# Query sets written and read in pairs, idle products, and the first feed-forward products inside the attention's end

## The reference

```python
x = x + layernorm(attention(layernorm(x), Wqkv, Wo))          # 32 heads of 16, one shared key and value head, ALiBi, causal
x = x + layernorm(ffn(layernorm(x), gate, up, down))          # weights of 4 bits, 512 -> 1376 -> 512
x = x + layernorm(layernorm(x) @ (weight * blockmask).T + bias)
x = x + layernorm(base + 0.5 * fourier(encode(layernorm(x))))  # folded into one 512 x 512 matrix

def ffn(x):      # Wg, Wu, Wd = (code - (zero + 1)) * scale, a zero and a scale for each group of 128 rows
    return (silu(x @ Wg) * (x @ Wu)) @ Wd
```

## Time and profile before

| | |
|---|---|
| median of 3 runs | 1154.56 us (1153.49 to 1155.82) |
| the profiled execution | 1155.38 us |
| its span, first to last instruction | 1153.6 us |
| PE busy | 1095.1 us, 95% of the span |
| DVE, ACT, POOL busy | 62%, 54%, 37% |
| mean granted clock of PE | 0.986 |

### The profile page before, as it was taken

One profiled execution on the slowest core, in us unless ns is written; L12 is line 12 of the kernel. 1 busy time (PEld: TensorE's weight loads), 2 busy tenths in 40 slices (PEclk: granted clock), 3 DMA queues, 4 the chain that ended last, 5 costly groups with the idle time before them and its releaser, 6 DMA issues.

```text
span 1153.6 us, 16292 instructions
## 1 busy us (share of the span) xinstructions
PE 1095.1 (95%) x5822; PEld 678.7 (59%) x5888; DVE 717.3 (62%) x1675; ACT 624.1 (54%) x1067; POOL 423.1 (37%) x494
## 2 busy tenths in 40 slices
PE   7699999999999999899998899999999999999997
PEld 7445346345334334334535667788878878777885
DVE  6597997996999999799622644251141151247674
ACT  5265875766778689987794434211111111136775
POOL 4364252354210634322265655221121121124765
PEclk8799999999999999999999999999999999999999
DMA  6416104003213012101310221330030032211101
GB/s 184 131 43 166 29 20 119 21 20 77 62 38 101 22 35 64 58 29 47 95 37 28 75 64 39 110 110 1 1 110 1 1 79 101 74 37 74 37 37 74
DMA packets 66349, 70.62 MB, mean 61 GB/s; under 512 B 39854, under 2 KB 45510, under 8 KB 64708
## 3 DMA queue, kind: packets, MB, share of 16 engines
q1 hardware_dynamic: 62540, 59.82, 17.4%
q0 software_dynamic: 3152, 8.63, 2.3%
q10 hardware_dynamic: 576, 1.11, 0.3%
HBM read 50.27 MB, written 18.87 MB: 60 GB/s over the span
## 4 chain that ended last, share of the span: by engine, by line
PE 78%; DVE 11%; ACT 5%; issue 2%; POOL 2%; DMA 1%; SPq 1%; POOLq 0%; DVEq 0%; ACTq 0%
PE PO L1511 10%; PE ST L1497 8%; PE bank L1413 8%; PE f_pair L61 7%; PE f_pair L63 7%; PE f_pair L62 7%; DVE bank L1207 3%; PE f_Y L1906 3%; PE f_Y L1908 3%; PE f_Y L1907 3%; ACT PT L1119 3%; PE l_psum L2331 2%; PE l_psum L2333 2%; PE l_psum L2332 2%; DVE mx L1209 2%
## 5 line engine op out<-in xcount | busy, mean ns | idle before, releaser
L1119 ACT ACTIVATE PT<-ST,lowered 128x512 f32<-128x512 f32 x576 | 355.1, 693 | 72.6 <-PE PO L1511 31.7
L1207 DVE CUSTOM_DVE_ANT_0 bank<-bank,tail_mask 128x512 f32<-128x512 f32 x320 | 211.1, 719 | 21.2 <-PE bank L1413 20.9
L1413 PE MATMUL bank<-KS,QS 125*128 125x512 bf16 (+2 forms) x896 | 179.4, 307 | 10.2 <-DMA QS<-q_scratch 4.7
L1497 PE MATMUL ST<-QS,KS 128*128 128x512 bf16 x523 | 170.2, 384 | 11.0 <-ACT PT L1119 4.3
L1209 DVE TENSOR_REDUCE mx<-bank 128x2 f32<-128x512 f32 (+2 forms) x256 | 161.1, 681 | 25.9 <-PE bank L1413 11.4
L1037 POOL TENSOR_SCALAR_AFFINE_SELECT PT<-PT 128x512 f32<-128x512 f32 x128 | 79.2, 646 | 220.3 <-ACT PT L1119 219.7
L1511 PE MATMUL PO<-PT,V 128*32 128x512 f32 x1152 | 152.6, 604 | 2.9 <-ACT OT L1132 1.7
L1832 DVE TENSOR_TENSOR f_h<-f_h,f_pair 128x512 f32<-128x512 f32 (+1 forms) x44 | 30.2, 687 | 194.8 <-ACT f_h L1776 194.8
L1776 ACT ACTIVATE f_h<-f_pair 128x512 f32<-128x512 f32 (+1 forms) x44 | 26.3, 598 | 217.1 <-PE f_pair L63 217.1
L1736 POOL TENSOR_TENSOR f_h_part<-f_h,f_h_part 128x512 fp32r<-128x512 f32 (+1 forms) x44 | 56.7, 1289 | 232.0 <-ACT f_h_part L1780 232.0
L61 PE MATMUL f_pair<-f_xT,gw 128*128 128x512 f32 (+1 forms) x352 | 139.9, 398 | 0.0
(11 more groups left out here) (210 smaller groups left out, 1799.0 us busy)
## 6 DMA issues: line engine op xcount, KB each, us to landing
QS<-q_scratch SPq DMA_DIRECT2D x96, 128.0 KB
q_scratch<-QP SPq DMA_DIRECT2D x36, 128.0 KB, 1.9
xres<-_attn_hidden_states_dram POOLq DMA_DIRECT2D x16, 256.0 KB, 3.3
x_dram<-xout POOLq DMA_DIRECT2D x16, 256.0 KB, 2.4
xin<-x_dram SPq DMA_DIRECT2D x4, 1024.0 KB, 7.7
f_xsum<-x_dram SPq DMA_DIRECT2D x4, 1024.0 KB, 7.0
x_dram<-f_xsum SPq DMA_DIRECT2D x4, 1024.0 KB, 4.7
out_dram<-l_xout SPq DMA_DIRECT2D x7, 512.0 KB, 2.8
```

What stands on the lines that cost most here:

```text
L1119: act.activation(PT[:, quad % PT_RING, n % 4, :], ST[:, n % ST_RING, :], ACT.Exp, bias=lowered[:, 0:1]).then_inc(p_done, 1)
L1207: v.tensor_tensor_reduce(at(u), at(u), tail_mask[:, :], 1.0, -3e38, ALU.add, ALU.max, mx[:, i % 2, z, h:h + 1]).then_inc(bank_free_dve, 1)
L1413: last = pe.matmul(at(u)[:, j * w:(j + 1) * w], QS[0:ROWS1, slot, h + j, :], KS[b][0:ROWS1, k0:k0 + w], start=(j == 0 or not diag), stop=( ...
L1497: pe.matmul(ST[:, n % ST_RING, :], KS[b][0:ROWS2, kb * P:(kb + 1) * P], QS[0:ROWS2, slot, h:h + 4, :], start=True, stop=True).then_inc(st_ ...
```

## The change

- **Sets.** The six sets stand in `QS` grouped by the query part (48 rows of part 0, then 32, then 16) and no longer interleaved, and a block's stack is three DMAs, each with a source that is read three, two or one times. `QP` is laid out by token tile, so that two groups m lie side by side, and a part is sent to `q_scratch` in pairs of m: six DMAs a piece in place of twelve, each of twice the bytes in runs of 512 B in place of 256 B. The key weights are copied in five groups rather than three. ACT, DVE and POOL write and read `QP` with a stride between token tiles.
- **Opening.** 13 products of zeros at the start in place of 12, and five more after the first two transposes. POOL waits with its second part of the weights (chunk 3) until DVE has done its first (`wx_lo` at 1).
- **The planner** knows of eight steps "ff" of three matmuls each, the gate and up products of tile 0 of block 0, which may run once all score tiles are issued and read, into banks 0 and 1 of `ST`, at the lowest rank. Its figures for SP's issues and the stacks are changed.
- **Feed-forward, block 0.** Tile 0's gate and up products are gone from it. Then follows one piece, and from tile 1 on gate, piece, up, piece, down of the tile before, piece. ACT takes silu between the copy and the high part of the second piece. DVE takes the row moments one tile of tokens at a time beside n = 1 to 4, and the normalising beside n = 5 to 8; it did all four beside n = 1 and n = 2. A gate or up product waits for the low parts of its weights chunk by chunk. Some counts of waits on SP are one lower.

```diff
-WARM_UP = 12
+WARM_UP, WARM_TURN = 13, 5
...
-def pieces_during(n):
-    p = n // 2 + 1
-    mine = [j for j, (u, _) in enumerate(DQ) if UNITS[u][0] == p]
-    return mine[0:3] if n % 2 == 0 else mine[3:6]
+def between(n):
+    extras = [("dq", j) for j, (u, _) in enumerate(DQ) if UNITS[u][0] > 0] + [("xt", t) for t in range(4)]
+    return extras[max(0, 3 * n - 2):3 * n + 1]
...
+        if at["ff"] < FF_STEPS and at["tile"] == 4 * QUADS:
+            m = at["ff"] // DC
+            made = [("dl", j) for j in EARLY_PIECES if UNITS[DQ[j][0]][1] <= m]
+            out.append((known(("read", 4 * QUADS - 1), ("xt", AFTER, 3), *made), free["pe"] + 9000, ("ff", at["ff"])))
...
-        KV_GROUPS = ((0, SETS, D), (SETS, 1, D + HD), (SETS + 1, P // HD - SETS - 1, D))
-        Q_OUT = 4 * 16
+        KV_GROUPS = tuple((PART_ROW[x] // HD, PART_SETS[x], D) for x in range(PARTS)) + ((SETS, 1, D + HD), (SETS + 1, P // HD - SETS - 1, D))
+        Q_OUT = 2 * 16
...
-                sp.dma_start(q_scratch[b, t:t + n, part, :, :, m].rearrange("t d h q -> (d h) t q"),
-                             QP[:, part, m, cols_of(k)].rearrange("p (t q) -> p t q", q=P)).then_inc(q_out[part], 16)
+                sp.dma_start(q_scratch[b, t:t + n, part, :, :, m - 1:m + 1, :].rearrange("t d h m q -> (d h) t (m q)"),
+                             QPv[:, part, tiles_at(k), m - 1:m + 1, :].rearrange("p t m q -> p t (m q)")).then_inc(q_out[part], 16)
...
-                for g in range(SETS):
-                    if Q_PART[g] == part:
-                        sp.dma_start(QS[g:SETS * HD:SETS, slot, :, :].rearrange("d h q -> d (h q)"),
-                                     q_scratch[b, qb, part].rearrange("d h m q -> d (h m q)")).then_inc(qs_in[slot], 16)
+                n, r = PART_SETS[part], PART_ROW[part]
+                sp.dma_start(QS[r:r + n * HD, slot, :, :].rearrange("d h q -> d (h q)"),
+                             q_scratch[b, qb, part].rearrange("d h m q -> d (h m q)").unsqueeze(1).to_broadcast([HD, n, NH * P])).then_inc(qs_in[slot], 16)
...
-            for m, part in ((0, 0), (1, 0), (0, 1), (0, 2), (2, 0), (1, 1), (1, 2), (3, 0), (2, 1), (2, 2), (3, 1)):
+            for m, part in ((1, 0), (1, 1), (1, 2), (3, 0), (3, 1)):
                 q_part_out(0, m, part)
             stack_part(0, 0)
             q_part_out(0, 3, 2)
...
             weights_low(0)
             piece_rstd(0)
+            pool.wait_ge(wx_lo, 1)
             weights_low(DC - 1)
...
+            def first_tile(x):
+                m, c = divmod(x, DC)
+                if x == 0:
+                    freed(pe, ("xt", AFTER, 3))
+                    pe.wait_ge(p_done, 4 * QUADS)
+                if c == 0:
+                    pe.wait_ge(dq.w_lo, pieces_before(0, m))
+                out = ST[:, m, :]
+                pe.matmul(out, hi(dq.gw[0][:, 0, m, c, 0:P]), hi(xT[0][:, c, :]), start=(c == 0), stop=False)
+                pe.matmul(out, hi(dq.gw[0][:, 0, m, c, 0:P]), hi(xT[1][:, c, :]), start=False, stop=False)
+                last = pe.matmul(out, hi(dq.gw[0][:, 1, m, c, 0:P]), hi(xT[0][:, c, :]), start=False, stop=(c == DC - 1))
+                if x == FF_STEPS - 1:
+                    last.then_inc(first_full, 1)
...
             for u in FIRST:
                 fill(u)
+                if u == ("xt", 0, 1):
+                    idle_products(WARM_TURN)
...
     for n in range(NT):
-        dq = [("dq", j) for j in pieces_during(n)] if blk == 0 else []
-        events += dq[0:1] + [("gate", n)] + dq[1:2] + [("up", n)] + dq[2:3]
+        if blk == 0:
+            x = between(n)
+            events += [("gate", n)] + (x[0:1] if n else []) + [("up", n)] + (x[1:2] if n else x)
+            events += [("down", n - 1)] + x[2:3] if n else []
+            continue
+        events += [("gate", n), ("up", n)]
...
         def banks(use):
-            return pair[:, SLOT_OF[use], :, :]
+            return att.first_banks if use == FIRST_GATE else pair[:, SLOT_OF[use], :, :]
...
+            silu(0, 0)
+            h_high(0, 0)
+            piece_or_rows(between(0)[0])
+            for n in range(1, NT):
+                x = between(n)
+                piece_or_rows(x[0])
+                piece_or_rows(x[1], then=n)
+                h_high(0, n)
+                piece_or_rows(x[2])
...
+                for n in range(NT) if blk == 0 else []:
+                    x = between(n)
+                    for y in x[0:2] if n else []:
+                        piece_or_rows(y)
+                    gated(0, n)
+                    if 1 <= n < 5:
+                        tile_moments(n - 1)
+                    elif 5 <= n < 9:
+                        normalize_tile(n - 5)
+                    for y in x[2:3] if n else x:
+                        piece_or_rows(y)
```

184 lines of the change are left out of this document (115 added, 69 removed).

## The result

The changed kernel takes 1144.67 us (median of 4 runs, 1143.62 to 1147.07) against 1154.03 for the one before: the ratio is 0.9919 with an interval of [0.9906, 0.9932]. It is faster, by 9.4 us where 22 were forecast, and it lies outside the range of 1124 to 1142. The profiled execution has a span of 1145.3 us, 8.3 less than before.

A forecast was written before the change was run, and what follows sets the result against it. PE was taken as the bound, the gain lying in its idle and slow-clock stretches: 10 us in the opening plus 13.2 at the attention's end and feed-forward's start, 23.2 in all, giving 1132 us, range 1124 to 1142.

The forecast's parts named there:

- Opening up to the low parts: Start to POOL's query low parts: earlier query products at full clock, together 3.0 us earlier, low part ready at 21.6.
- SP's queue: Opening, last send's wait for issue on SP: 0.6 us kept of 3.47, as fewer sends and stack issues stand ahead.
- The landings I leave at 2.85 and 2.49 us: Opening, last send and last stack DMA: landing times kept despite the doubled send; ends 1 us less, 2 us more.
- rival 4: Stack DMAs reading one source three times run on fewer engines; from half the rate only the opening pays, some 4 us; chance 0.03.
- Score tiles: Opening, first score tiles waiting for the maxima's DMAs: three stack issues for six ahead, 2.0 us taken of 2.3.
- Clock, 1.5 + 2.0: Opening, slow clock behind the waits for first scores and first score tiles: 1.5 of 2.2 and 2.0 of 2.6 us regained.
- The end: Attention's end and feed-forward's start: 13.2 us saved by filled waits and reordered pieces, ends 8 and 14.
- Filled waits, 5.6: Attention's end: eight steps in PE's waits save 4.0 of 4.64 us, and output products at full clock 1.6 us.
- Second piece, "+0.3": Feed-forward's start: the second piece waits for the first one's product on DVE, behind silu, costing 0.3 us.
- First down product, "+0.5": Feed-forward's start: it cannot start before 639.1 because of POOL's late start, costing PE a 0.5 us wait.
- The batch, 3.8 + 1.5: Feed-forward's start: row tiles one at a time on DVE remove waits of 3.8 us and 1.5 us of slow clock.
- The middle: Middle of the attention, its order planned anew: gain taken as 0, with 3 us to either side.

The follow-up runs named there:

- e9: Against the changed kernel with old stack loading, later residual loads and last send first (1135.59 us): all four row tiles' moments and normalisations batched again; 1137.73 us.
- e16: Changed kernel with old stack loading, later residual loads, last send first, first piece before silu, first h's low part on DVE, two pauses filled; 1132.24 us.

## Why the prediction was wrong

**The sign and the path held; the landings failed, and two more terms of the opening with them.** *Opening up to the low parts:* right. POOL's wait freed DVE (1.10 us for 2.41, the products of the rows' low parts done at 11.98), the queries run at full clock and end 2.9 us earlier for the 3.0 forecast; the low part is ready at 21.8 for 21.6. The second chunk of DVE took 1.47 us and not 1.09 beside POOL's, as the Trainium skill's rule cited there had it (behind POOL's end at 12.35, 1.09 us more would be 13.44; it ended at 13.37):

```profile
9.63 1.10 DVE L1351 TENSOR_TENSOR wx<-PT,wx 128x512 fp32r<-128x512 f32 x1
...
11.90 1.47 DVE L1351 TENSOR_TENSOR wx<-PT,wx 128x512 fp32r<-128x512 f32 x1
```

```profile
10.81 1.54 POOL L1022 TENSOR_TENSOR wx<-PT,wx 128x512 fp32r<-128x512 f32 x1 [2.13 <-DVE wx L1351]
```

*SP's queue:* right, 0.9 us from the low part to the issue for 0.6. *"The landings I leave at 2.85 and 2.49 us":* the step that failed. The send took 7.87 us, the stack behind it 2.9, together 5.4 of the 5.9 us by which the first scores missed 27.6. The bound of 2 us more had been put there for twice the bytes. Two things that were in view had no part in the sum: the stack's new rows and form, weighed only in rival 4, and POOL's residual loads. Before, the last send was issued 3.5 and 2.8 us behind these loads, and they had landed or nearly so. Now most of the wait in SP's queue is gone, the send is issued 0.9 and 0.2 us behind them, and both are still under way. *Score tiles, "half of 4.62, of which I take 2.0":* three issues take 3.20 us and not 2.3, as each is longer, and the maxima's DMAs behind them 6.0. *Clock, 1.5 + 2.0:* not given back, since the waits ahead grew to 7.5 and 5.3 us. Landings that grow, and the clock of 0.5 behind the first scores, are two of the four signs that the prediction named for being wrong.

**Rival 4** had the mechanism in its text ("from half the rate only the opening pays, some 4 us") but as fewer engines, at 0.03, and without its hold on the send and on the maxima. With both it costs 5.5 to 7.5 us at the first tile, 4.1 to 6.6 in the medians. The Trainium skill's rule on the number of engines (DMA: Bandwidth & Descriptors, "Why a DMA increments its semaphore by 16 and not by 1"), cited there, is not contradicted, with sixteen and more packets in flight. It was the wrong rule to rest the chance on: the packets in flight were as many, and each took longer.

**The end,** 13.2 forecast and 10.1 measured. *Filled waits, 5.6:* 5.65 by the rows; but all eight steps stood ahead of the last output products, not six, so these end only 0.7 us earlier against the shift and not 1.6, and POOL's start with them. *Second piece, "+0.3":* 1.48; the prediction did not add up ACT's line, though the trace of before has every duration in it (the table's load was 1.28 us at 636.89). *First down product, "+0.5":* 0.65. *Not foreseen:* 0.82 us ahead of a down product near 739 and two waits of 0.37 and 0.32 near 690. Together 1.2 + 0.1 + 0.8 + 0.7 = 2.8 of the 3.1. *The batch, 3.8 + 1.5:* the sum was right, the reason mostly not (e9).

**The middle** was forecast at 0 within 3 us: 1.1 us less.

That e16 comes out at 1132.2 does not mend the forecast: it has six edits that the change hasn't (stack, residual loads, the send's place, the first piece, the low part, filled pauses).

## What to carry to other kernels

When a change brings a transfer forward, list what is on the DMA engines at the new time, from every queue, before its old landing time is kept: here loads that nobody waited for took 4 us. Price a DMA's new shape by its rows on the SBUF side, not by bytes, packets or issues alone; here neighbouring rows in place of spread ones made a packet a quarter to two fifths longer, and with a source read several times on top half as long again. And a pause of about 2 us costs itself and, in some executions, as much again in clock. Two waits of 1.48 and 0.65 us left the clock full where one of 2.31 lost it, and unused products in the pauses paid.
